# Who adds the residual to the dense product beside the scan: an identity matmul and a ScalarE copy in place of VectorE's addition

## What is computed

```
h      = ctx (4 x 1024 x 512) projected to 1024 channels, causal conv of 4 taps, SiLU   -> u
delta  = softplus(dt_proj(x_proj(u)));  B, C = x_proj(u)       (16 states per channel)
state  = state * exp(delta * A[:, n]) + (delta * u) * B[n]     for n = 0..15, scanned over 1024 steps
y      = sum over n of state * C[n]  + D * u,  times silu(layernorm(x))
x      = x + y
xn     = layernorm(x)
out    = x + xn @ W_base.T + b_base + sum of the 2 chosen experts (rank 8 each), gated
```

## Time and profile before

| | us |
|---|---|
| median of 3 runs | 2097.69 (2096.14 to 2099.48) |
| profiled execution, its own time | 2104.84 |
| profiled execution, span from first to last instruction | 2103.0 |
| VectorE busy | 1787.7 |
| TensorE busy | 1782.0 |
| GpSimd busy | 1767.9 |
| ScalarE busy | 1256.7 |

### The profile page before, as it was taken

The page is one execution under the profiler, slowest core; times in us unless marked ns, Lnnn a source line. Parts: engine busy times, 40 slices in busy tenths (PEclk is TensorE's granted clock), DMA queues, the critical chain, the costliest instruction groups (busy, mean ns, idle before and its releaser), DMA issues.

```text
span 2103.0 us, 23735 instructions
## 1 busy us (share of the span) xinstructions
PE 1782.0 (85%) x7996; PEld 1094.4 (52%) x7996; DVE 1787.7 (85%) x1432; ACT 1256.7 (60%) x1701; POOL 1767.9 (84%) x796
## 2 busy tenths in 40 slices
PE   8767777877788899889989899899888888888999
PEld 3344554545455555555655555555555555555554
DVE  3589999999899999998989999988989999997111
ACT  3346655555666766766666666766666666663431
POOL 0279999999999999999989999999999999997200
PEclk9788778778779999999989999999999999989999
DMA  4565555576756666697755566686665666565200
GB/s 153 216 251 186 200 198 193 196 244 234 281 197 197 228 217 214 216 320 257 245 194 192 213 217 210 207 310 243 237 206 199 212 200 215 196 214 214 108 30 30
DMA packets 157977, 435.88 MB, mean 207 GB/s; under 512 B 14528, under 2 KB 47552, under 8 KB 157728
## 3 DMA queue, kind: packets, MB, share of 16 engines
q1 hardware_dynamic: 157856, 434.37, 60.2%
HBM read 383.46 MB, written 50.86 MB: 207 GB/s over the span
## 4 chain that ended last, share of the span: by engine, by line
DVE 39%; PE 29%; issue 17%; POOL 7%; ACT 5%; DMA 3%; DVEq 0%; SPq 0%; POOLq 0%; ACTq 0%
DVE state L1055 23%; DVE row L1040 10%; PE bank_a L545 8%; PE y_ps L489 6%; POOL prod L1194 5%; DVE conv L1032 3%; PE bank_b L545 3%; PE row L567 3%; PE row L483 2%; PE bank_b L449 2%; PE bank_a L556 1%; ACT decay L809 1%; PE bank_b L440 1%; POOL drive_rows L1187 1%; DMA xrow<-in_x 1%
## 5 line engine op out<-in xcount | busy, mean ns | idle before, releaser
L1194 POOL TENSOR_TENSOR prod<-state,c_rows 128x1024 f32<-128x1024 f32 x512 | 1200.3, 2359 | 91.8 <-DVE state L1055 40.3
L1055 DVE TENSOR_TENSOR_SCAN state<-decay,row 128x1024 f32<-128x1024 f32 x334 | 762.8, 2284 | 7.4
L489 PEld LDWEIGHTS y_ps<-ident,prod 128*128 128x128 f32 x4096 | 520.2, 152 | 296.2 <-issue 189.8
L489 PE MATMUL y_ps<-ident,prod 128*128 128x128 f32 x4096 | 592.5, 294 | 44.2 <-POOL prod L1194 41.2
L1040 DVE TENSOR_TENSOR row<-du,row 128x1024 f32<-128x1024 f32 x334 | 404.3, 1210 | 41.6 <-PE row L483 37.7
L809 ACT ACTIVATE row<-delta,a 128x1024 f32<-128x1024 f32 x178 | 199.0, 1118 | 379.9 <-DVE state L1055 379.0
L1187 POOL TENSOR_TENSOR drive_rows<-du,b_rows 128x1024 f32<-128x1024 f32 x178 | 420.9, 2365 | 1.9 <-DMA b_rows<-bc_d 1.9
L1055 DVE TENSOR_TENSOR_SCAN state<-row,drive_rows 128x1024 f32<-128x1024 f32 x178 | 404.7, 2274 | 17.9 <-POOL drive_rows L1187 16.8
L545 PE MATMUL bank_a<-w_o,xnT 128*128 128x512 f32 x816 | 402.0, 625 | 18.1 <-DVE x L1102 18.1
L809 ACT ACTIVATE decay<-delta,a 128x1024 f32<-128x1024 f32 x334 | 374.1, 1135 | 0.0
L483 PE MATMUL row<-parts,sel 96*128 96x512 bf16 x668 | 223.6, 419 | 173.9 <-DVE state L1055 171.6
(11 more groups left out here) (131 smaller groups left out, 1636.8 us busy)
## 6 DMA issues: line engine op xcount, KB each, us to landing
c_rows<-bc_d SPq DMA_DIRECT2D x512, 512.0 KB, 4.4
xrow<-in_x SPq DMA_DIRECT2D x32, 512.0 KB, 7.1
skip<-u_d SPq DMA_DIRECT2D x32, 512.0 KB, 6.0
yy_d<-yy SPq DMA_DIRECT2D x32, 512.0 KB, 6.3
b_rows<-bc_d SPq DMA_DIRECT2D x24, 512.0 KB, 8.5
u_d<-conv SPq DMA_DIRECT2D x24, 512.0 KB, 5.3
ctx<-u_d SPq DMA_DIRECT2D x48, 256.0 KB, 5.8
x<-in_x SPq DMA_DIRECT2D x24, 512.0 KB, 5.9
```

The source lines that it names most:

```text
L489: last = nc.tensor.matmul(y_ps[:, i * P:(i + 1) * P], source[:, i * P:(i + 1) * P], ident[:, :], start=(first and i % (H // P) == 0), stop ...
L1055: nc.vector.tensor_tensor_scan(state[:, q % STATES, :], factor, term, 0.0, ALU.mult, ALU.add).then_inc(scan_done, 1)
L1194: nc.gpsimd.tensor_tensor(prod[:, q % PRODS, :], state[:, q % STATES, :], c_rows[:, q % RING, :], ALU.mult).then_inc(prod_ready, 1)
```

## The change

For the dense tiles beside the scan (`single` is true for them) each half's PSUM group now begins with a matmul of the identity against x in SBUF, 128x128 by 128x512, in float32, so that x is already in the sum. ScalarE then copies the finished bank over x in SBUF and counts `res_ready` up. VectorE's two additions per tile are gone. ScalarE's copies stand at the same sections, m = 13 (behind the decays of n = 14 and 15 and ahead of the row sum) and m = 1 of the next block (ahead of the copies of dt's half tiles). The tail's nine tiles keep VectorE's addition.

```diff
@@ TensorE, product(j, h, ks, at, single)
+                if 0 in ks and single:
+
+                    nc.tensor.matmul(at.sums[h][:, :], ident[:, :], x1_place(j)[:, half(h)], start=True, stop=False)
                 for k in ks:
-                    nc.tensor.matmul(at.sums[h][:, :], at.xnT[:, k, :], w_o[:, k, half(h)], start=(k == 0), stop=False)
+                    nc.tensor.matmul(at.sums[h][:, :], at.xnT[:, k, :], w_o[:, k, half(h)], start=(k == 0 and not single), stop=False)
@@ ScalarE
+            def take_result(j, h, at):
+                act.wait_ge(o_ready, 2 * j + h + 1)
+                nc.scalar.activation(x1_place(j)[:, half(h)], at.sums[h][:, :], ACT.Copy).then_inc(res_ready, 1)
@@ ScalarE, section(E, m)
                 if m == 0:
                     scale_skip(E)
+                if m == 1 and j >= 1:
+                    take_result(j - 1, 1, beside)
...
                     table(LOGEXP)
+                if dense and m == 13:
+                    take_result(j, 0, beside)
                 if j >= -1:
                     if m == 13:
                         row_sum(j + 1)
@@ ScalarE, after the last block
+            take_result(FIRST_TAIL - 1, 1, beside)
@@ VectorE, section(E, m)
-                if m == 1 and j >= 1:
-                    add_residual(j - 1, 1, beside)
...
-                if dense and m == 13:
-                    add_residual(j, 0, beside)
@@ VectorE, after the last block
-            add_residual(FIRST_TAIL - 1, 1, beside)
```

## The result

| | before | changed |
|---|---|---|
| median, us | 2098.59 (4 runs, 2096.14 to 2100.28) | 2153.45 (4 runs, 2153.05 to 2153.82) |
| ratio, 95% interval | | 1.0268 (1.0254 to 1.0282) |
| profiled execution, own time / span, us | 2104.84 / 2103.0 | 2153.57 / 2151.8 |

The change costs 54.9 us, 2.7%. The forecast was 2120.7 us, with a range up to 2138: the sign was right, and the forecast loss of 23.0 us is less than half of what came. The spans of the two profiled executions differ by 48.8 us only, since the one of before was slow among its kind. The changed kernel's four runs lie within 0.8 us.)

The account below looks back on a forecast made before the run. TensorE's product up to row 15, directly ahead of VectorE's drive of n = 15, was taken as the bound in each block. 19.8 + 18.8 + 7 - 15.6 - 7 = 23.0 us on 2097.69 gave 2120.7 us, range 2103.5 to 2138.

Parts of the forecast that it names:

- The step to row 15: At m = 13, TensorE's later start (18.8 us) and half 1's identity (19.8 us) delay row 15 and drive 15.
- the hand-over at m = 13: TensorE waits for ScalarE's copy behind the decays of n = 14 and 15: 18.8 us over the dense blocks.
- half 1's identity: One matmul between the wait at m = 13 and row 15, 0.86 us at full clock: 23 x 0.86 = 19.8 us.
- block 27's kind: Nine blocks, two half tile ones among them, where TensorE would start 1.04 us later at m = 13: 9.4 us.
- the third rival: Longer waits at m = 13 put identity and three matmuls at half clock, nine blocks: 31 us more, 2151.7; chance 0.12.
- The argument against that rival: Blocks 10 and 13 wait nearly 3 us yet stay at full clock; extra matmuls leave TensorE less idle elsewhere.
- The term at m = 6: Half 0's identity delays rows 8 or 10 and their drives: 7 us taken, bounds nothing and 10.1 us.
- The swallowing: GpSimd's backlog at block ends absorbs a shift of about 1 us in one block of three: -7 us, bounds 0 and 14.
- The gain at m = 1: VectorE's removed additions give 13.0 us, and scan 1's vanished wait for GpSimd's drive 2.6 us: -15.6 us together.
- The base: The profiled 2104.84 us keeps its 7.15 us distance to the median, so the whole difference is added to 2097.69 us.
- The rule of the Trainium skill: First rival: relieving VectorE, the busiest engine, of 27.1 us gives 2070.6 us, or 2084.7 counting only m = 1; chance 0.08.
- The second rival: GpSimd sets the pace everywhere, so shifts at m = 15 and the gain vanish: within 4 us of 2097.69; chance 0.07.

Follow-up runs that it names:

- half 1 alone: Kernel before with only half 1 changed (identity matmul at m = 13, ScalarE's copy at m = 1), VectorE's addition kept for half 0: 2110.59 us, ratio 1.0065.
- ScalarE's copies alone: Changed kernel with the identity matmuls left out, so x is missing from the dense tiles' result: 2106.77 us, ratio 1.0039 to the kernel before.
- with the wait filled: Changed kernel plus two unused TensorE matmuls ahead of the wait for ScalarE's copy at m = 13, last eight dense blocks: 2144.18 us, ratio 1.0220.
- the best form of the change: Changed kernel with ScalarE's half 0 copy ahead of the decays and identities behind their half's eight matmuls: 2090.28 us, repeated 2091.21 us.

## Why the prediction was right in sign and wrong in size

**The step to row 15 was right.** The prediction put the loss at the hand-over at m = 13 and half 1's identity on the path to row 15, at 38.6 us. The last stretch grew by 41.2. In the blocks with three half tiles both terms came almost exactly, 0.64 for 0.57 and 0.86 for 0.86. One reading was too wide: in blocks 10, 13, 22, 25, 27 and 29 of the kernel before, scan 14 ended 0.2 us after row 15, and drive 15, 0.09 us behind the row, did not wait for it. Row and scan were ready together there, so a later row still moved the drive.

**The sum of that step was right partly by luck.** In the nine blocks of block 27's kind I expected 1.90 us each. Blocks 25, 27 and 29 show 3.87 (6.0 to 9.88): the wait grew from the earlier trace rows's 1.02 us to 1.53, and the identity and part of the product ran at half the clock, as in the third rival. It had a chance of 0.12 and a price of 31 us over nine blocks, 3.44 each; that priced the six records at 2.58 us more, where the earlier trace rows had shown 1.54. What came, against the full clock, was 2.06 us in each of the blocks 25 to 30 and 1.5 to 2.5 in most others of the two half tile and no half tile kinds. On the other side the kernel before had paid for half clock as well, as in block 26, and where it had, the step cost only 0.8 to 1.2 us (8.68 to 9.88). If every last stretch had been as short as those at the full clock (6.3 and 6.0 us before, 7.81 after), it would have grown by 39.4 us, against the 38.6 of the prediction; half clock and other waits added 28.9 us before and 30.7 after. So the two nearly cancelled in this stretch, which I had not foreseen, and not in the blocks.

The argument against that rival was picked too narrowly. It named blocks 10 and 13, which wait nearly 3 us and keep the full clock. Blocks 18 and 21 of the same trace have the same wait of 2.81 us and half clock behind it. Blocks 13 and 18, from the end of scan 12 to drive 15 (columns as above):

```profile
887.78:893.79 6.01, 4.24 (x17) 2.54 (x18) 6.01 (x6) 5.90 (x9) 6.01 (x4) 1.00 0.21 87
1183.85:1192.79 8.94, 7.18 (x17) 3.81 (x18) 6.08 (x4) 7.64 (x12) 8.94 (x5) 0.62 0.36 140
```

The length of the wait alone doesn't tell whether the clock falls; what does stays open.

**The term at m = 6 was mis-sized.** I took 7 us and gave 10.1 as the upper bound; the two middle stretches grew by 18.1 us. The bound priced the matmul at the full clock, 0.86 us. In block 27 it took 1.70 (from its start at 1710.81 to that of the next matmul, 1712.51), and drive 8 waited 0.87 us. So it went in blocks 24 to 30, and these seven hold 11.3 of the 18.1 us. The clock makes the difference: with VectorE's copy in ScalarE's place the same identity took 0.86 us, at a granted clock of 1.00, in blocks 24 to 29, and the two stretches together changed by only 0.3 us over these six. That TensorE can start m = 6 at half the clock in such a block was to be read in the trace of before, whose block 27 has, in time:

```profile
1676.03 0.74 PE L483 MATMUL row<-parts,sel 96*128 96x512 bf16 x2 [2.80 <-DVE state L1055]
...
1676.56 3.49 PE L545 MATMUL bank_a<-w_o,xnT 128*128 128x512 f32 x4
```

After a wait of 2.80 us the four records take 3.49 us, where four at the full clock take 1.88. I had not priced that.

**The swallowing was wrong.** I let GpSimd's backlog swallow 7 us. No sign of it is there: with half 1 alone, and with ScalarE's copies alone, where nothing was added at m = 6, the last stretch grew by 7.5 and 15.6 us and the two middle ones did not shrink but grew, by 3.7 and 1.3. Where blocks of 53.3 and 56.0 us alternated, all six from 25 to 30 became 58.03 to 58.08 us long, with GpSimd busy for 93%. As I read it, once VectorE is late by more than GpSimd's rest in a block, there is no backlog at the next block to draw on; that is argued and not shown. I had applied the backlog seen in the kernel before to a kernel that no longer had it. VectorE, too, had more rest in a block than the "about 2 us" of the prediction: 3.8 us in block 26.

**The gain at m = 1** was 12.0 us, against 13.0 for the additions and 2.6 for the drive's wait. That wait did go, from 2.7 us to none, but VectorE's waits for rows in the same stretch grew from 6.0 to 9.4 us.

**The base.** I moved the whole difference of the profiled execution onto the median. The kernel before varied by 17 us over its 56 further runs and its profiled execution was a slow one; the changed kernel varied by 0.8 over four and its profiled execution was typical. That is 6.1 us (54.9 by medians, 48.8 by spans). A kernel whose slow stretches come and go has no single profile to add to.

**The steps that failed,** then, are the term at m = 6 (7 us taken, 18.1 measured; it was priced at the full clock only, and 11.3 of the 18.1 us lie in the seven blocks that met it at half the clock), the swallowing (7 us taken, none seen) and the base (6.1 us); the terms of the last stretch and of m = 1 were off by 2.6 and 3.6. By size: predicted +23.0, plus 2.6 (last stretch), 3.6 (m = 1), 11.1 (m = 6), 7 (swallowing), 1.5 (outside) gives 48.8, and 6.1 for the base gives 54.9.

**The rivals.** The rule of the Trainium skill (Perfetto Trace Analysis, Identifying the Most-Contended Engine), that the engine with the highest occupancy be relieved first, gave 2070.6 or 2084.7 us. The busiest engine was relieved by 24 us of busy time and the kernel lost 54.9 us; the measurement decides against the rule here, where three engines stood within 20 us of busy time and the addition moved onto the engine that the busiest one waited for. The second rival, GpSimd's pace, is out for the change by its waits for the scans, 93.5 us. The third was part of the answer: half clock came as it said, but in this stretch it added only 1.8 us to what the kernel before had paid, and the larger part came at m = 6, of which it said nothing. The Trainium skill (TensorE: Matmul & The Clock Gate, HAM oscillation) says that a loop which leaves TensorE idle for long enough in each round is throttled in each round; the page's case is a wait for a DMA. The blocks 25 to 30 agree in that the clock fell in every one of them, with 9.87 us from scan 12 to drive 15 against 7.80 in the three that kept the clock with the wait filled. They do not show that the wait for the copy did it, since the clock fell before. Block 24 waited 2.01 us for the copy at a granted clock of 1.00, and the seven blocks with three half tiles kept the full clock as well.

## What to carry to other kernels

When several engines are busy for the same share, don't ask which is the busiest but whose instruction starts last behind which; here one place per block (drive 15 directly behind row 15, by 0.04 to 0.09 us) told the sign of the change. When a buffer's release moves to another engine, its place in that engine's order matters more than the work moved: two lines higher on ScalarE were worth 47.6 us, and one line higher on VectorE, in the kernel before, as much as the best form of the change. Price a matmul that follows waits at half the clock as well as at the full one, and those behind it too: at m = 13 of block 27 that was 2.06 us instead of none, at m = 6 0.84. And look at where the clock fell before you blame the wait in front of the slow matmul. Last, ask what the freed engine will wait for next: here much of what VectorE could have gained at m = 1 went into a wait for GpSimd.

## What the runs showed of the hardware that was not expected

Two extra 512-column matmuls in each of eight blocks, ahead of a wait that was 1.5 us long in most of them, made the kernel 9.3 us faster (2144.18 against 2153.45). From scan 12 to drive 15 the granted clock was 1.00 in three of the blocks 25 to 30 and 0.81 in the others, where it had been 0.65.

The same wait of 2.81 us went with a granted clock of 1.00 in blocks 10 and 13 of the kernel before and of 0.62 in blocks 18 and 21.

The kernel before varied from 2091.4 to 2108.7 us over 56 runs, the changed one from 2153.05 to 2153.82 over 4. The changed kernel's last dense blocks are alike to 0.05 us, each with the same half clock stretch. That the kernel before varies because its half clock stretches fall differently from run to run fits the traces but was not tested.
